# Attention, MLP and layer norm on one core: new durations in the table that orders the engines' work

## What is computed

```python
q = (hidden_states @ Wq.T)                       # 32 heads of 128
c_kv = hidden_states @ Wdk.T                     # low-rank keys and values, 8 kv heads
...
scores = jnp.einsum('bhqd,bhkd->bhqk', q, k) * scale
causal = jnp.tril(jnp.ones((q_len, q_len), bool))
scores = jnp.where(causal[None, None], scores, jnp.asarray(-1000000000.0, dt))
attn = jax.nn.softmax(scores, axis=-1)
out = jnp.einsum('bhqk,bhkd->bhqd', attn, v)
...
return out @ Wo.T
```

## Time and profile before

| | |
|---|---|
| median of 3 executions | 2416.55 us (2415.39 to 2419.6) |
| the profiled execution | 2418.7 us, span from first to last instruction 2416.8 us |
| mean granted clock of TensorE | 0.993 of full speed |
| busy in the span: PE, PEld | 97%, 82% |
| busy: DVE, ACT, POOL | 61%, 47%, 39% |
| second stage | from about 604 us to the end |

### The profile page before, as it was taken

One profiled execution on the slowest core, in us unless ns is written; L12 is line 12 of the kernel. 1 busy time (PEld: TensorE's weight loads), 2 busy tenths in 40 slices (PEclk: granted clock), 3 DMA queues, 4 the chain that ended last, 5 costly groups with the idle time before them and its releaser, 6 DMA issues.

```text
span 2416.8 us, 35041 instructions
## 1 busy us (share of the span) xinstructions
PE 2341.2 (97%) x11840; PEld 1972.8 (82%) x11840; DVE 1477.3 (61%) x3641; ACT 1133.3 (47%) x2217; POOL 939.3 (39%) x813
## 2 busy tenths in 40 slices
PE   6999999999899999999999999999999999999998
PEld 5777877777788888888888888888888888888877
DVE  5343343424676766666676767666766667666765
ACT  3452524335454544445444545454544445454544
POOL 1000000000554554545454545455454545454543
PEclk9999999999999999999999999999999999999999
DMA  5676757789412121221212152312212131303110
GB/s 194 187 283 189 254 176 227 263 264 335 157 44 106 44 97 62 88 98 43 105 44 105 36 191 82 129 44 96 78 72 105 36 114 36 112 29 114 35 53 18
DMA packets 103810, 286.56 MB, mean 119 GB/s; under 512 B 9072, under 2 KB 42352, under 8 KB 92528
## 3 DMA queue, kind: packets, MB, share of 16 engines
q1 hardware_dynamic: 101552, 280.53, 34.1%
q10 hardware_dynamic: 2112, 4.19, 0.5%
HBM read 200.80 MB, written 83.89 MB: 118 GB/s over the span
## 4 chain that ended last, share of the span: by engine, by line
PE 70%; DVE 3%; issue 2%; ACT 2%; DMA 1%; POOL 1%; SPq 1%; POOLq 0%; ACTq 0%; DVEq 0%
PE ob L1093 16%; PE scores L1067 15%; PE qb L1048 14%; PE ob L1108 13%; PE ptb L1079 10%; DVE pT L1009 1%; DMA ff_raw<-in_ffw 1%; PE ring L844 1%; PE ring L829 1%; SPq L556 1%; ACT long_prob L951 1%; ACT pT L966 1%; PE down L853 0%; DVE q_sin L1004 0%; DVE q_sin L1003 0%
## 5 line engine op out<-in xcount | busy, mean ns | idle before, releaser
L966 ACT ACTIVATE pT<-ptb 128x512 fp32r<-128x512 f32 x576 | 335.5, 594 | 506.7 <-PE ptb L1079 504.1
L1093 PE MATMUL ob<-pT,v_sb 128*128 128x512 f32 x1728 | 476.3, 405 | 7.0 <-DVE pT L1009 7.0
L1009 DVE TENSOR_TENSOR pT<-ptb,pT 128x512 fp32r<-128x512 f32 x576 | 390.8, 688 | 96.0 <-ACT pT L966 92.3
L937 POOL TENSOR_TENSOR q_cos<-q_cos,q_sin 128x512 f32<-128x512 f32 x125 | 161.9, 1295 | 559.8 <-DVE q_cos L1005 559.8
L931 POOL TENSOR_TENSOR long_prob<-long_prob,rinv 128x384 f32<-128x384 f32 (+3 forms) x256 | 304.7, 1203 | 171.4 <-DVE rinv L1027 171.4
L1048 PE MATMUL qb<-xT,wq 128*128 128x512 f32 x1488 | 358.2, 390 | 0.0
L1093 PEld LDWEIGHTS ob<-pT,v_sb 128*128 128x128 f32 x1728 | 304.2, 188 | 59.5 <-DVE pT L1009 13.7
L931 POOL TENSOR_TENSOR short_prob<-short_prob,rinv 128x512 f32<-128x512 f32 (+3 forms) x256 | 278.4, 1095 | 189.0 <-DVE rinv L1027 186.2
L1067 PE MATMUL scores<-kT,late_qT 128*128 128x384 f32 (+3 forms) x1536 | 343.9, 359 | 0.0
L1048 PEld LDWEIGHTS qb<-xT,wq 128*128 128x128 f32 x1488 | 279.3, 188 | 59.5
L1067 PEld LDWEIGHTS scores<-kT,late_qT 128*128 128x128 f32 x1536 | 264.3, 188 | 27.5 <-POOL late_qT L941 4.0
(11 more groups left out here) (95 smaller groups left out, 2994.4 us busy)
## 6 DMA issues: line engine op xcount, KB each, us to landing
wq<-w_parts SPq DMA_DIRECT2D x126, 512.0 KB, 3.6
w_parts<-stage SPq DMA_DIRECT2D x32, 1024.0 KB, 4.9
ff_raw<-in_ffw SPq DMA_DIRECT2D x56, 384.0 KB, 3.8
k_parts<-stage SPq DMA_DIRECT2D x128, 128.0 KB, 2.3
v_parts<-stage SPq DMA_DIRECT2D x64, 256.0 KB, 3.6
w_raw<-in_wqo SPq DMA_DIRECT2D x32, 512.0 KB, 5.7
kT<-k_parts SPq DMA_DIRECT2D x16, 1024.0 KB, 7.4
v_sb<-v_parts SPq DMA_DIRECT2D x16, 1024.0 KB, 8.8
```

What stands on the lines that cost most here:

```text
L937: nc.gpsimd.tensor_tensor(qc, qc, qs, ALU.add).then_inc(q_turned, 1)
L966: nc.scalar.activation(pT[:, t % 4, HI], ptb[t % 2][:], ACT.Copy).then_inc(pT_hi, 1)
L1009: nc.vector.tensor_tensor(pT[:, t % 4, LO], ptb[t % 2][:], pT[:, t % 4, HI].bitcast(F32), ALU.subtract).then_inc(pT_split, 1)
L1093: mm = nc.tensor.matmul(ob[:], v_sb[e % 2][:, x, j], pT[:, t % 4, y], start=(j == 0 and (x, y) == (HI, HI)), stop=(is_last(kind, n, j) and ...
```

## The change

Only the durations in `followers` differ, of EXP, INV, NORM and of all parts of Q but ACT's, each with the time after it until the result may be used:

```diff
     if kind == "S":
-        return [("dve", "S", n, j, 1.04 * cols + 0.08, 0.1), ("act", "EXP", n, j, 0.98 * cols + 0.15, 0.2),
-                ("dve", "INV", n, j, 0.12, 0.06), ("pool", "NORM", n, j, 1.83 * cols + 0.03, 0.05)]
+        return [("dve", "S", n, j, 1.04 * cols + 0.08, 0.1), ("act", "EXP", n, j, 0.86 * cols + 0.29, 0.1),
+                ("dve", "INV", n, j, 0.14, 0.06), ("pool", "NORM", n, j, 1.66 * cols + 0.19, 0.05)]
     if kind == "Q":
-        return [("dve", "Q", n, j, 1.97, 0.05), ("pool", "Q", n, j, 1.1, 0.1),
-                ("act", "QL", n, j, 0.55, 0.1), ("pool", "QL", n, j, 1.1, 0.1)]
+        return [("dve", "Q", n, j, 2.01, 0.08), ("pool", "Q", n, j, 1.29, 0.05),
+                ("act", "QL", n, j, 0.55, 0.1), ("pool", "QL", n, j, 1.29, 0.05)]
```

## The result

| | before | changed |
|---|---|---|
| median | 2418.07 us (4 runs, 2415.39 to 2420.49) | 2436.87 us (4 runs, 2434.87 to 2438.25) |
| ratio | | 1.0077, 95% interval 1.006 to 1.0095 |
| profiled execution, span | 2416.8 us | 2435.1 us |
| mean granted clock | 0.993 | 0.994 |

The change costs 18.8 us. The forecast was 2436.7 us. That it is met within 0.2 us is luck: the loss in the medians is 1.4 us smaller than the forecast 20.2, and a fourth run of the kernel before has raised its median from 2416.55 by 1.5.

A forecast was written before the change was run, and what follows sets the result against it. PE, busy 97% of the span, was taken as the bound. Terms 20.2 + 0 + 0.1 = 20.3, say 20.2, put the profiled 2418.7 us at 2438.9; less 2.15 for the median, 2436.7 us, range 2433 to 2442.

The forecast's parts named there:

- What bounds the kernel: Second stage: PE, busy 111.07 of 111.80 us in eight steps, has no idle time to make up a wait.
- The place: Step 8k+4, 16 times: QL(8k+7) behind NORM(8k+4, 0) on POOL makes PE's load for S(8k+4, 3) 1.26 us later.
- The price: Per step 8k+4, one NORM of 640 columns, 1.25 us, plus 0.01: 1.26 us, 16 times, 20.2 us.
- The upper bounds of the terms: Main term 21.9 us, opening 1.2, step 8k+8 1.5, and 2 for the median of few runs.
- What is queued behind: Step 8k+4: later PE work shifts by 1.26 us, DVE's INV ahead of S and T's slack of 0.35: costed at 0.
- the cover: Step 8k+4: the late load hides DVE's swap; without it T would wait 0 to 0.3 us, at most 5 us.
- The other moves: Reorderings in step 8k+8 on DVE (bounds 0 and 1.5 us), 8k+1 on POOL and 8k+3 on DVE: each 0.
- the opening: Once at the start: POOL's chain some 0.1 us later, S(0, 1)'s 1.2 us wait hidden: +0.1, bounds -0.5 and +1.2.
- Rival 1: PE's sixteen waits of some 1.4 us lower its clock: 2463 us if every time, 2445 if once in three; chance 0.06.
- Rivals 2 to 4: T late by DVE's order, 2438 to 2441.5 us, chance 0.06; PE's wait not QL's, no change, 0.04; DVE waits shrink, 0.02.
- Rival 4: Step 8k+3: swapping INV and S on DVE shortens PE's `pT` wait, up to 7.0 us, 2409.6 us; chance 0.02.

The follow-up runs named there:

- e5: Kernel before with NORM(8k+4, 0) and NORM(8k+4, 1) put ahead of QL(8k+7) on POOL, 16 times: 95.9 us over the kernel before.
- e2: Kernel before with only NORM(8k+4, 0) put ahead of QL(8k+7) on POOL, 16 times: 20.1 us over the kernel before.
- e1: Changed kernel with only POOL's move undone, QL(8k+7) ahead of NORM(8k+4, 0) again: 4.4 us over the kernel before.
- e3: Kernel before with only INV(8k+4, 2) put ahead of S(8k+4, 3) on DVE, 16 times: 5.0 us over the kernel before.
- e4: Changed kernel with both moves in steps 8k+4 undone (POOL's QL and NORM, DVE's INV and S): 1.3 us over the kernel before.
- e6: Kernel before with T(8k+2, 1) put ahead of S(8k+3, 2) in PE's order, 16 times: 4.7 us faster than the kernel before.

## Why the prediction was right

- *What bounds the kernel.* PE without slack: e5 shows that a wait is never made up.
- *The place.* The move of QL behind NORM(8k+4, 0) was named as the one that matters, and alone it gives the loss (e2) and the wait rows to the last digit.
- *The price.* 1.26 us was worked out. PE loses 1.20 in eight steps (e2, and the changed kernel without the one wait for `wo_b`; 1.28 with it), and the timeline shows a load that waits 1.49 us instead of the forecast 1.51: NORM 1.25 and QL 1.27 instead of 1.29, and POOL started the NORM 0.09 us after the reciprocal instead of 0.08. The sum of 20.2 compares with 18.8 in the medians and with 19.2 by the eight steps of e2. In the 20.5 of the changed kernel's trace the one wait for `wo_b` counts for 1.0. From the first S to the end its trace is 20.0 us longer (608.91 to 2435.1, before 610.65 to 2416.8), and its first stage 1.7 us shorter. So the price is some 5% high, and the medians come nearer to the forecast time than the terms do. The upper bounds of the terms (21.9, 1.2, 1.5 and 2 us) add to 2443 and not to 2442, which changes nothing.
- *What is queued behind* at 0: held beside the late QL (the rows above that answer to the earlier trace rows). The side remark that DVE's swap alone would hold the maximum from 889.52 to 890.68 was borne out in e1 and e3; the prediction put it at 5 us at most were the cover gone, and 4.4 and 5.0 came (3.2 by the traces); it was the 7 us in the expectations of e1 and e3 that were too high.
- *The other moves* at 0, and 0.1 for the opening. e4 agrees. In the opening S(0, 1) does wait for QL(1), 1.2 us on the load as forecast and 0.83 on the matmuls, and the longer wait behind it hides that: it shrinks from 4.79 to 4.41 us. The 0.44 us wait of the first T for a NORM goes, and its wait for `pT` grows from 1.07 to 1.56 us, which is the whole growth of that row. The first late load comes 55.3 us after the first S instead of 54.1, the 1.24 us of that load and nothing more:

```profile
613.42 0.96 PE L1067 MATMUL scores<-kT,early_qT 128*128 128x512 f32 x3 [0.83 <-POOL early_qT L941]
626.12 3.32 PE L1067 MATMUL scores<-kT,early_qT 128*128 128x384 f32 x9 [4.41 <-DVE nmax L988]
```

- *Rival 1, the clock.* It didn't fall at 1.2 us, 16 times of 16 by the windows behind the waits, and did at 3.9, 16 of 16. The mechanism is real; it didn't come at this length. Its condition of once in three at 2.05 us also held: in the twelve traces 11 of the 36 such waits in the first stage are followed by 48 matmuls in 12.78 to 12.83 us, the other 25 by the same in 11.15 to 11.19. By the rule of the Trainium skill (TensorE: Matmul & The Clock Gate, "A second HAM failure mode: psum-queue depth-cycling"), taken from one other kernel, frequent short idles make the clock swing: no run here with waits of 0.2 to 1.3 us bears that out.
- *Rivals 2 to 4* didn't come. Rival 4's wait for `pT`, 7.0 us, could be removed, but by PE's order (e6) and not by the swap on DVE that the change brought.

**Why durations nearer to the trace made a worse list.** The planner's own clock, printed at step 20, says when POOL's two items become ready (its us, not the chip's):

```
table before:  QL(23) 284.430   NORM(20, 0) 284.482
table changed: QL(23) 287.888   NORM(20, 0) 287.856
```

A lead of 0.052 became one of -0.032. POOL is free at that moment, the planner gives it whatever is there first, and a NORM isn't interrupted. On the chip QL led by 0.04 us (886.85 against 886.89). The planner makes this swap with EXP's new numbers alone, not with those of EXP, INV and NORM together, and again with all of them: it hangs on hundredths. EXP's result at 640 columns comes 0.04 us sooner by the new formula (0.86 x 0.64 + 0.29 + 0.1 = 0.94, before 0.98 x 0.64 + 0.15 + 0.2 = 0.98). The planner decides a near tie by arrival. Of the two items one has PE waiting behind it; the other still has slack when it stands second: NORM(8k+4, 0) then ends at 889.42, 0.26 us before POOL's next NORM starts, and T has another 0.35.

## What to carry to other kernels

An order made by a planner is only as good as its near ties: look in the new list for each pair that changed places, find in the trace which of the two has the bounding engine waiting behind it, and the price is the length of the item that went ahead, times its repetitions, as long as the waiting engine has no slack and the wait is not so long that its clock falls. Better durations don't help a planner that decides by arrival; who is waited for must be in its priorities. And a move that wins at one wait has to be run alone before it is added to others: of three that each aimed at a wait of PE, two won 10 us together and the third lost 5.

## What the hardware showed beyond the forecast

A wait of 3.92 us of TensorE costs about 2.1 us more in lowered clock (at the place shown 0.57 granted in the next 4 us, and six matmuls in 1.96 us instead of 1.14), more than the 1.63 us read from the first stage; one of 1.23 us costs nothing more. In between lies a chance and no fixed price. The waits of 2.05 us were followed by slower matmuls in 11 cases of 36. Of the wait of 1.49 us at the start of the first stage, once in each of the twelve traces, the 48 matmuls behind took 13.17, 14.06 and 13.19 us in three (before, e3, e6) and 11.15 to 11.19 in nine. The granted clock reads 1.00 there in both cases, so the cause of these three stays open; they come behind 14 us of idle time and 16 short matmuls, and are no measure of a wait amid dense work. They do account for 2 to 3 us between runs of one kernel, as much as some effects above.

And a reordering that is free beside one stall (DVE's INV ahead of S, with QL late) costs 0.20 us in eight steps without it: effects of moves don't simply add.
